# A sliding-window attention layer with a ternary feed-forward on eight cores: V product split in two, transposes emptied by ScalarE alone, Q, K and V passes in one block

## The reference

```python
x = x + attn(layernorm(x))
x = x + ffn(layernorm(x))

def attn(h):                              # rmsnorm without weights other than 1, rope by position
    q, k, v = split(h @ Wqkv, 3)
    q, k = rope(rmsnorm(q)), rope(rmsnorm(k))
    mask = (q_idx >= k_idx) & (q_idx - k_idx <= 1023)
    probs = softmax(where(mask, q @ k.T / sqrt(128), -inf))
    return (probs @ v) @ Wo

def ffn(h):                               # ternary: +-0.5 beyond 0.33, +-0.6 beyond 0.2, else 0
    return ternary(h, 0.33, 0.5) @ (ternary(weight, 0.2, 0.6) + rram_variation).T
```

## Time and profile before

| | |
|---|---|
| two timed runs, median | 3338.55 us (3329.24 and 3347.85) |
| profiled execution | 3303.83 us |
| its span, slowest core (core 2) | 3302.0 us |
| spans of all cores | 3268.7 to 3302.0 us |
| mean granted TensorE clock, all cores | 0.666 to 0.670 |
| busy in the span: TensorE, VectorE, ScalarE | 55%, 23%, 23% |
| DMA traffic | 156.09 MB, mean 47 GB/s |

### The profile page before, as it was taken

The page is one execution under the profiler, slowest core; times in us unless marked ns, Lnnn a source line. Parts: engine busy times, 40 slices in busy tenths (PEclk is TensorE's granted clock), DMA queues, the critical chain, the costliest instruction groups (busy, mean ns, idle before and its releaser), DMA issues. The chain is left out here.

```text
span 3302.0 us, 28275 instructions; the slowest of 8 cores (3268.7 to 3302.0 us)
## 1 busy us (share of the span) xinstructions
PE 1812.3 (55%) x8448; PEld 850.4 (26%) x8448; DVE 746.8 (23%) x1764; ACT 745.5 (23%) x1248; POOL 90.4 (3%) x153
## 2 busy tenths in 40 slices
PE   1225777213355227777589778878977446213333
PEld 0112333001122113333245334434533112001111
DVE  1111000054311240000331331233131211332222
ACT  3551111722100411111122122212313000332222
POOL 0000000000000001111000000000000000000000
PEclk9999888655587658888555555555555668556666
DMA  3211111000122002221200000000000333014343
GB/s 103 77 64 58 51 52 45 0 0 0 58 70 77 0 20 77 80 79 56 53 7 1 7 7 7 1 7 7 1 7 20 98 106 83 0 47 125 114 122 103
DMA packets 72820, 156.09 MB, mean 47 GB/s; under 512 B 12992, under 2 KB 12992, under 8 KB 70368
## 3 DMA queue, kind: packets, MB, share of 16 engines
q1 hardware_dynamic: 62016, 120.61, 12.4%
q0 software_dynamic: 10656, 33.67, 3.5%
HBM read 137.47 MB, written 16.78 MB: 47 GB/s over the span
## 5 line engine op out<-in xcount | busy, mean ns | idle before, releaser
L411 PE MATMUL psA<-wchunk,R 128*128 128x512 bf16 x1280 | 331.6, 416 | 280.6 <-DVE wchunk L394 280.6
L247 PE MATMUL psD<-identb,ropeo 128*128 128x128 bf16 x320 | 84.3, 263 | 544.4 <-DVE ropeo L495 263.6
L411 PE MATMUL psB<-wchunk,R 128*128 128x512 bf16 x1280 | 294.1, 383 | 0.0
L411 PEld LDWEIGHTS psA<-wchunk,R 128*128 128x128 bf16 x1280 | 131.2, 104 | 464.0 <-issue 335.7
L874 PE MATMUL psA<-wchunk,R 128*128 128x512 bf16 x256 | 67.7, 425 | 222.3 <-DVE wchunk L860 222.2
L247 PEld LDWEIGHTS psD<-identb,ropeo 128*128 128x128 bf16 x320 | 33.5, 105 | 596.3 <-issue 596.3
L251 ACT COPY R<-psD 128x128 bf16<-128x128 bf16 x384 | 102.1, 266 | 352.0 <-PE psC L247 285.8
L394 DVE CAST wchunk<-wstgA 128x512 bf16<-128x512 f32 x96 | 41.0, 427 | 578.8 <-PE psB L411 421.5
L651 PE MATMUL psA<-R 128*128 128x128 bf16 x576 | 166.0, 288 | 9.9 <-ACT wstgB L631 9.9
L411 PEld LDWEIGHTS psB<-wchunk,R 128*128 128x128 bf16 x1280 | 127.2, 99 | 158.2 <-issue 12.8
L651 PE MATMUL psB<-R 128*128 128x128 bf16 x576 | 166.2, 288 | 0.0
(11 more groups left out here) (117 smaller groups left out, 2339.9 us busy)
## 6 DMA issues: line engine op xcount, KB each, us to landing
wstgA<-wqkv SPq DMA_DIRECT2D x96, 256.0 KB, 2.7
wstgB<-wqkv SPq DMA_DIRECT2D x96, 256.0 KB, 2.8
wchunk<-x_all SPq DMA_DIRECT2D x16, 1024.0 KB, 4.8
vhbm<-PTb POOLq DMA_DIRECT2D x64, 128.0 KB, 2.1
R<-vhbm POOLq DMA_DIRECT2D x16, 512.0 KB, 6.0
wstgA<-wo SPq DMA_DIRECT2D x32, 256.0 KB, 3.1
wstgB<-wo SPq DMA_DIRECT2D x32, 256.0 KB, 3.2
R<-x_all POOLq DMA_DIRECT2D x32, 256.0 KB, 3.2
```

Source lines behind the costliest of these rows:

```text
L247: tv = pl.op("tensor", lambda e, s=slot, x=src_ap: e.transpose(s, x, identb[:]), sem=ct)
L411: ctm = pl.op("tensor", lambda e, d=d, t=t, ps=ps: e.matmul(ps, xlnT[:, lhs_col(t, d):lhs_col(t, d) + 128], wchunk[:, 512 * d:512 * (d + 1 ...
```

## The change

Five edits:

- `emit_PV` runs 9 matmuls of 128 columns of V and then 9 matmuls with a moving operand of one column (`validb`), on the same stationaries, into column 128 of the same bank. The slots of the ring become 2048 columns wide, `ring_validcol` goes, and a ring load is 128 rows of 4096 bytes where it was 128 x 16 pieces of 256 bytes. TensorE itself waits for the ring load, ahead of `emit_ST(0)`.
- All heads use psC; a product waits until the one before it is emptied.
- `TrPipe.do` has every transpose emptied by ScalarE, whichever slot it lies in.
- `qkv_pass` waits once for all 16 casts of a chunk.
- P2k, P3q and P4v become one block. The guards of the staging buffers, of psA and psB and of the last matmul are carried over in `QS`.

```diff
         def do(self, pl, src_ap, dst_ap, scale=None):
             si = self.idx % 2
-            eng = "scalar" if si == 0 else "vector"
-            ctr = cs if si == 0 else cv
...
             if self.guard[si] is not None:
-                gc, gv = self.guard[si]
-                pl.wait("tensor", gc, gv)
+                pl.wait("tensor", cs, self.guard[si])
             tv = pl.op("tensor", lambda e, s=slot, x=src_ap: e.transpose(s, x, identb[:]),
                        sem=ct)
-            pl.wait(eng, ct, tv)
-            if scale is None and si == 0:
+            pl.wait("scalar", ct, tv)
+            if scale is None:
                 g = pl.op("scalar", lambda e, s=slot, dd=dst_ap: e.copy(dd, s),
                           ins=[slot], out=dst_ap, sem=cs)
...
+    QS = {"stg": [None, None], "par": [None, None], "prev": None}
...
-        stg_guard = [None, None]
-        par_guard = [None, None]
-        prev_mm = None
+        stg_guard = QS["stg"]
+        par_guard = QS["par"]
+        prev_mm = QS["prev"]
...
-                if d == 7:
-                    cast_mid = stg_guard[si]
-            cast7 = cast_mid
             cast15 = stg_guard[1]
+            pl.wait("tensor", cv, cast15)
             for ti, t in enumerate(tiles):
...
-                if ti == 0:
-                    pl.wait("tensor", cv, cast7)
...
-                    if ti == 0 and d == 8:
-                        pl.wait("tensor", cv, cast15)
...
-    p.run("P2k")
...
-    p.run("P3q")
...
-    ldv0 = None
     for l in range(NKT):
-        ldv0 = ring_dma(l)
-    p.wait("vector", RNG, ldv0)
-    for l in range(NKT):
-        ring_validcol(l)
+        ring_ld[l] = p.dma("gpsimd",
+                           vring[:, 2048 * (l % NKT):2048 * (l % NKT) + 2048],
+                           bass.AP(vhbm.tensor, l * 128 * D, [[D, 128], [1, 2048]]), RNG)
...
             p.wait("gpsimd", ct, ring_guard[j - 1])
-            ldv = ring_dma(j + 8)
-            p.wait("vector", RNG, ldv)
-            ring_validcol(j + 8)
+            ring_ld[j + 8] = p.dma(
+                "gpsimd", vring[:, 2048 * sl:2048 * sl + 2048],
+                bass.AP(vhbm.tensor, (j + 8) * 128 * D, [[D, 128], [1, 2048]]), RNG)
...
-        p.wait("tensor", cv, ring_ld[j + 8])
+        p.wait("tensor", RNG, ring_ld[j + 8])
...
-            if psc_guard[par] is not None:
-                p.wait("tensor", cs, psc_guard[par])
+            if psc_guard is not None:
+                p.wait("tensor", cs, psc_guard)
+            for l in range(NKT):
+                sl = (j + l) % NKT
+                p.op("tensor", lambda e, PT=PT, l=l, sl=sl, h=h: e.matmul(
+                    psC[:, 0:128], PT[:, 128 * l:128 * (l + 1)],
+                    vring[:, 2048 * sl + 128 * h:2048 * sl + 128 * (h + 1)],
+                    start=(l == 0), stop=(l == NKT - 1)))
             ctpv = None
             for l in range(NKT):
-                sl = (j + l) % NKT
-                vr = bass.AP(R1.tensor, VSL * sl + 129 * h, [[34960, 128], [1, 129]])
-                ctpv = p.op("tensor", lambda e, pc=pc, PT=PT, l=l, vr=vr: e.matmul(
-                    pc[:, 0:129], PT[:, 128 * l:128 * (l + 1)], vr,
-                    start=(l == 0), stop=(l == NKT - 1)),
+                ctpv = p.op("tensor", lambda e, PT=PT, l=l, j=j: e.matmul(
+                    psC[:, 128:129], PT[:, 128 * l:128 * (l + 1)],
+                    validb[:, j + l:j + l + 1], start=(l == 0), stop=(l == NKT - 1)),
                     sem=(ct if l == NKT - 1 else None))
```

More of the change, by code:

```diff
@@ L162, in build_nc @@
     sba = lambda n, s, d: nc.alloc_sbuf_tensor(n, s, d).ap()
-    R1 = sba("R1", [128, 34960], BF16)
+    R1 = sba("R1", [128, 34816], BF16)
     R2 = sba("R2", [128, 32768], BF16)
@@ L193, in build_nc @@
     psDb = nc.alloc_psum_tensor("psD", [128, 1024], BF16).ap()
-    psC2 = psDb.bitcast(F32)
     psCb = psC.bitcast(BF16)
     xlnT = R1
-    cosb = R1[:, 32912:33936]
-    sinb = R1[:, 33936:34960]
+    cosb = R1[:, 32768:33792]
+    sinb = R1[:, 33792:34816]
     vring = R1
-    VSL = 2064
-    o_sb_base = NKT * VSL
+    o_sb_base = NKT * 2048
     kT = R2
@@ L425, in qkv_pass @@
             prev_mm = ctm
+        QS["prev"] = prev_mm
         return ev
@@ L468, in postprocess @@
         tr2 = TrPipe()
-        prev_tr = None
+        prev_tr = QS.get("pp_prev_tr")
         for t in tiles:
@@ L502, in postprocess @@
             prev_tr = ct.v
+            QS["pp_prev_tr"] = prev_tr
     p = Plan(nc, OWN)
@@ L512, in build_nc @@
                 ev_k, 3, tq_of=lambda t: t)
-    p.run("P2k")
-    if kphases < 3:
-        return _finish_early()
-    p = Plan(nc, OWN)
     def q_dst(t, ci):
@@ L622, in build_nc @@
                 p.wait("tensor", cs, nm2_prev)
-                if psc_guard[1] is not None:
-                    p.wait("tensor", cs, psc_guard[1])
             tv = None
@@ L692, in emit_PV @@
             p.wait("vector", ct, ctpv)
-            rcv = p.op("vector", lambda e, pc=pc, h=h: e.reciprocal(
-                rinv[:, h:h + 1], pc[:, 128:129]), ins=[pc[:, 128:129]],
+            rcv = p.op("vector", lambda e, h=h: e.reciprocal(
+                rinv[:, h:h + 1], psC[:, 128:129]), ins=[psC[:, 128:129]],
                 out=rinv[:, h:h + 1], sem=cv)
@@ L697, in emit_PV @@
             oc = o_col(j, h)
-            psc_guard[par] = p.op("scalar", lambda e, pc=pc, h=h, oc=oc: e.activation(
-                out=R1[:, oc:oc + 128], in_=pc[:, 0:128], func=AF.Copy,
-                scale=rinv[:, h:h + 1]), ins=[pc[:, 0:128], rinv[:, h:h + 1]],
+            psc_guard = p.op("scalar", lambda e, h=h, oc=oc: e.activation(
+                out=R1[:, oc:oc + 128], in_=psC[:, 0:128], func=AF.Copy,
+                scale=rinv[:, h:h + 1]), ins=[psC[:, 0:128], rinv[:, h:h + 1]],
                 out=R1[:, oc:oc + 128], sem=cs)
@@ L719, in build_nc @@
     cs_oT = cs.v
-    cv_oT = cv.v
     p.wait("tensor", cs, cs_oT)
-    p.wait("tensor", cv, cv_oT)
     xres_guard = [None, None, None, None]
@@ L820, in build_nc @@
     cs_xqT = cs.v
-    cv_xqT = cv.v
     p.run("P7ln2")
@@ L865, in build_nc @@
             p.wait("tensor", cs, cs_xqT)
-            p.wait("tensor", cv, cv_xqT)
         for j in range(NQ):
```

31 lines of the change are left out of this document (5 added, 26 removed).

## The result

The changed kernel takes 3229.8 us (median of 11 runs) against 3310.7 us for the kernel before, run beside it: ratio 0.974, 95% interval 0.971 to 0.978, so 2.6% faster. A later measurement gave 0.980 (0.976 to 0.984), which leaves open whether the gain is above 2%. I had forecast 3311, in a range from 3255 to 3375. In some executions of any kernel here the cores of one die show a lower granted clock and take some per cent longer; the ratios leave these executions out, the medians in us don't.

A forecast was written before the change was run, and what follows sets the result against it. TensorE was taken to bound attention, at half its full clock, and waits for weight staging, transposes or statistics to bound the other stages. The terms summed to -27.9 us on 3338.55, giving 3311 us, range 3255 to 3375.

The forecast's parts named there:

- one-column pairs: Attention's V product: 1152 added pairs of weight load and one-column matmul at 0.06 us each, +69 us.
- ring waits: Attention: VectorE no longer waits for V ring loads before a query tile's first maximum, -70.9 us.
- one PSUM bank: Attention's V products in one bank: nothing waits, and the last head's added pairs cost less, -1 us.
- wait for all 16 casts: First tile of each of 12 weight chunks: 8 matmuls start later, 1.69 us each chunk, +20.2 us.
- three blocks in one: Seams K to Q and Q to V: casts start 9.6 and 9.9 us earlier, -19.6 us.
- transposes on ScalarE: Norm and rotary stages: +8.6 us over 24 norm tiles, -5.3 us in rotary, sum +3.3 us.
- the same ahead of Wo: Before the output projection: VectorE casts Wo while ScalarE empties transposes, removing most of TensorE's idle 29.80 us, -29.0 us.
- P1's term: Norm stage P1: each tile's last transpose copy on ScalarE delays the next statistics by 0.36 us, +5.7 us.
- the ring wasn't late: Rival in attention: late ring loads only move the wait to TensorE, net +43, 3382 us; chance 0.03.
- both dearer prices of the pairs: Rivals in attention: 0.106 us a pair, set by weight loads, 3364 us, chance 0.20; 0.216 without overlap, 3491 us, 0.09.
- the higher clock: Rival in attention: without pauses, TensorE gets full clock for a fifth of the stage, -78 us, 3233 us; chance 0.06.
- the forecast's own lower bound: Attention's one-column pairs, from weight loads 0.03 us apart: 35 us for the pairs, -62 in all, 3277 us; chance 0.07.

The follow-up runs named there:

- group doubled: The changed kernel with a second, unread group of nine one-column matmuls per head, in the next column of the same bank: 3296.7 us, ratio 0.997.
- fused again: The changed kernel with 129-column V products again, V stored in HBM with its valid columns, no VectorE wait for the ring: 3219.9 us, ratio 0.974.
- combined version: The changed kernel with V products fused without VectorE's wait, the wait for cast 7 put back, and both PSUM banks for products: 3198.1 us, ratio 0.967.
- mid-chunk wait back: The changed kernel with the waits for cast 7 and cast 15 of each Q, K and V chunk put back: 3206.9 us, ratio 0.970.
- transposes alone: The kernel before with one edit, every transpose emptied by ScalarE: 3287.5 us, ratio 0.994.
- Padding before: The kernel before with 1152 idle, unread one-column matmuls at the head of TensorE's list in P8ffn: 3301.6 us, ratio 0.996.

## Why the prediction was wrong

| term | forecast | measured | by |
|---|---|---|---|
| one-column pairs | +69.1 | +27 to +29 | group doubled; fused again |
| ring waits | -70.9 | -70.5 | the two traces |
| one PSUM bank | -1 | +2 to +4 | second pass; combined version |
| wait for all 16 casts | +20.2 | +22 | mid-chunk wait back |
| three blocks in one | -19.6 | -20 | mid-chunk wait back against before |
| transposes on ScalarE | +3.3 | +7 | transposes alone |
| the same ahead of Wo | -29.0 | -27 | transposes alone |
| sum | -27.9 | about -58 | |

The ring's -70.5 is read from before and after: on the cores' first query tile the maximum pass went from 54.0 to 22.9 us (core 2), on each later one from 28.2 to 22.6.

**The step that failed** is "0.06 us looks like the floor of a pair that isn't held by its columns". I had read it off the first two transposes after an idle spell. Nothing in that row says that these two stood in the queue together and ready; two starts 0.06 us apart bound the pace from above only. The changed kernel shows the same thing inside a queue: the first step of a group of nine takes 0.070 us, the seven after it 0.027. The same group of rows held the better number: two weight loads 0.03 us apart. I named it as the lower end and then chose the far one. That is worth 40 us: +69.1 in the sum, 27 to 29 measured. The Trainium skill ("TensorE: Matmul & The Clock Gate", LDWEIGHTS) gives a load its columns over 1.2 GHz, an estimated 0.107 us for 128 of them. The duration of a load agrees (113 ns in the mean), the pace doesn't: 0.027. The Trainium skill also says, in the section "Wait — 56ns, not 53.3ns?" of the same page, that start to start never drops below about 25 ns however few the columns, with an example at the higher clock; with 1 and 16 columns at 1.2 GHz this case shows 0.025 to 0.027, and that agrees.

**The base** was wrong too: I put the change on the median of two runs, 3338.55 us, although the profiled execution of the same kernel stood at 3303.8. In 10 runs the median is 3310.7. This is 28 us of the 81 between forecast and result. On the profiled execution's base the forecast would have been 3276, and the measured kernel 46 us below it.

**The rest.** The terms measured sum to -58, the steps of the profiles to -61, and the timed medians differ by 81 in the first measurement and by 65 in the second. So 7 to 23 us of gain are nobody's term. In the profile 5.4 of them are Wo's matmuls. Padding before to the changed kernel's 81 packets shortened the same stages by 11 us and the time by some 13, though its profile shows 9 us lost in other passes. That makes the length of the program, or what changes with it, a likely cause of part of it, not a shown one.

**What came as forecast.** The first maximum follows the first scores at once; the ring loads are never late; a chunk of the three passes is 1.8 us longer (1.69), though the first tile itself, 5.40 us in the median where I had 3.37 + 1.69 = 5.06, scatters by 2 us; the seams between the passes are 20.1 us shorter; TensorE doesn't wait ahead of Wo; a pair of transposes takes 53.8 / 64 = 0.84 us. The sign of a query tile's change was wrong: from 115.0 to 113.1 us, not 3 longer, since pairs and bank cost 3.8 and the wait had been worth 5.7. The bank's term had the wrong sign. From a tile's second-last product to its last it is 2.87 us (1680.34 to 1683.21), 2.42 before; 0.24 of the difference are the pairs, so the wait for the copy costs 0.2 us a query tile where I had it save 0.12. P1's term was 2 us short, 0.48 us a tile where I had 0.36; why is open.

Of the rivals, the ring wasn't late, and both dearer prices of the pairs were on the wrong side. The one rival below the sum, the higher clock, had 3233 us, within 4 us of the measured time, but by accident: the clock didn't rise (0.51 against 0.50). What came true was the forecast's own lower bound, two starts 0.03 us apart: its -62 us is the change of the profiles, -61. At 0.07 for it I had given it too little.

## What to carry to other kernels

Price a small instruction by the spacing of starts in a row of many like ones, never by the duration of one and not by one gap after a pause; if the profile only bounds it, centre the sum between the bounds and let both decide the chances. A wait for a transfer has two prices, where the wait stands and how fast the transfer is, and an edit may change both. Check a base of two runs against the profiled execution, and compare stages rather than whole times: a kernel whose stages were otherwise the same moved by 35 us when idle instructions were added.

## What the runs showed of the hardware

- On TensorE at 1.2 GHz, pairs of a 128x128 weight load and a matmul of 1 or 16 columns start 0.025 to 0.027 us apart in a row of like ones, the first step after a longer matmul taking 0.07; with 64 columns the steps are 0.053 us (0.50 for nine pairs), with 129 columns 0.106. The loads last 0.10 to 0.15 us each and overlap.
- 1152 such pairs with nothing between them stood idle after every 128th, up to 3.8 us, and took 38 to 43 us.
- A ring load of 512 KB in pieces of 4096 bytes ends a wait 2.3 us sooner than the same in pieces of 256 bytes (3.9 against 6.2 us of waiting), and nine of them in a row 13.6 us sooner. GpSimd took 0.52 us to issue the former and 1.15 the latter, and paused 13 us after seven of these.
- The median loads of 256 KB to all eight cores for Wo and the feed-forward took 2.9 to 3.6 us in one profile of the changed kernel, 2.9 to 4.2 in another, and 3.4 to 4.8 in a kernel that differs by 1152 hidden matmuls. The combined version with that padding is the fastest kernel of the study, 3180.7 us, but the padding is no advice: the same edit costs 35 us in the changed kernel.
